# Latent layers with a couple's own projections between its rounds, and the first up-projections of three MLPs beside the last attention rounds

## The reference

```
attn = einsum(q, k) * scale, masked;  attn = softmax(attn)
out  = attn @ v @ out_w + out_b + residual
u    = rmsnorm(out, postnorm_w)              # layers 0 and 3
y    = gelu(u @ mlp_w1 + mlp_b1) @ mlp_w2 + mlp_b2 + residual
```

## Time and profile before

| | us |
|---|---|
| median of three runs | 2559.47 (2557.16 to 2562.12) |
| the profiled execution's own time | 2562.53 |
| its span | 2560.7 |
| PE busy in the span | 2452.8 |
| DVE, ACT, POOL busy | 1231.4, 1085.6, 1120.2 |

### The profile page before, as it was taken

The page is one execution under the profiler, slowest core; times in us unless marked ns, Lnnn a source line. Parts: engine busy times, 40 slices in busy tenths (PEclk is TensorE's granted clock), DMA queues, the critical chain, the costliest instruction groups (busy, mean ns, idle before and its releaser), DMA issues.

```text
span 2560.7 us, 48767 instructions
## 1 busy us (share of the span) xinstructions
PE 2452.8 (96%) x18464; PEld 2053.4 (80%) x18464; DVE 1231.4 (48%) x3296; ACT 1085.6 (42%) x3712; POOL 1120.2 (44%) x1972
## 2 busy tenths in 40 slices
PE   7999998999999999998888999999999999899999
PEld 6888886888888878886777788888888888788887
DVE  4555655332224667766666332243455556432332
ACT  4555554111114787777767111111455555311111
POOL 2453545600053787778876630033344443730000
PEclk9999999999999999998988999999999999999999
DMA  4111312211033233223443320122021111320100
GB/s 162 59 59 59 104 55 79 83 50 50 1 109 126 74 106 121 96 97 125 150 161 121 115 91 1 50 87 74 26 88 63 51 43 61 114 87 1 50 33 17
DMA packets 106774, 198.07 MB, mean 77 GB/s; under 512 B 8304, under 2 KB 35632, under 8 KB 103600
## 3 DMA queue, kind: packets, MB, share of 16 engines
q1 hardware_dynamic: 106544, 194.97, 23.1%
HBM read 136.22 MB, written 58.72 MB: 76 GB/s over the span
## 4 chain that ended last, share of the span: by engine, by line
PE 79%; ACT 11%; DVE 5%; POOL 3%; issue 1%; DMA 1%; SPq 0%; DVEq 0%; POOLq 0%
PE banks L326 70%; ACT plain_high L731 5%; PE banks L467 5%; PE banks L497 3%; ACT plain_low L731 2%; POOL plain_high L1342 2%; ACT plain_work L796 1%; DVE stats L1134 1%; PE banks L521 1%; ACT plain_work L715 1%; DVE plain_work L1149 0%; DMA plain_high<-attention_w 0%; DVE plain_high L1004 0%; ACT plain_low L715 0%; DVE rounded_low L1053 0%
## 5 line engine op out<-in xcount | busy, mean ns | idle before, releaser
L326 PE MATMUL banks<-rounded_work,rounded_low 128*128 128x512 f32 (+1 forms) x2688 | 534.3, 355 | 11.5 <-DVE rounded_low L1166 9.5
L326 PEld LDWEIGHTS banks<-rounded_work,rounded_low 128*128 128x128 f32 x2688 | 445.3, 198 | 76.8 <-issue 15.9
L982 ACT ACTIVATE plain_work<-banks,columns 128x512 f32<-128x512 f32 x192 | 132.4, 690 | 870.8 <-PE banks L326 870.8
L326 PE MATMUL banks<-rounded_work,rounded_high 128*128 128x512 f32 (+1 forms) x2400 | 483.4, 355 | 2.1 <-DMA rounded_work<-ctx_split 1.7
L326 PEld LDWEIGHTS banks<-rounded_work,rounded_high 128*128 128x128 f32 x2400 | 396.6, 191 | 68.2 <-issue 6.2
L1342 POOL TENSOR_SCALAR plain_high<-plain_high,inv_sum 128x128 f32<-128x128 f32 (+1 forms) x768 | 296.6, 409 | 317.5 <-DVE inv_sum L1026 317.2
L1318 DVE CAST rounded_work<-plain_work 128x512 fp32r<-128x512 f32 x192 | 105.3, 549 | 685.7 <-ACT plain_work L982 674.9
L326 PE MATMUL banks<-rounded_low,rounded_work 128*128 128x512 f32 x1728 | 414.9, 391 | 0.0
L326 PE MATMUL banks<-rounded_high,rounded_work 128*128 128x512 f32 (+1 forms) x1728 | 390.2, 377 | 0.0
L326 PEld LDWEIGHTS banks<-rounded_low,rounded_work 128*128 128x128 f32 x1728 | 321.6, 188 | 68.6 <-issue 2.8
L326 PEld LDWEIGHTS banks<-rounded_high,rounded_work 128*128 128x128 f32 x1728 | 309.1, 188 | 60.5 <-issue 1.4
(11 more groups left out here) (106 smaller groups left out, 3120.9 us busy)
## 6 DMA issues: line engine op xcount, KB each, us to landing
plain_work<-x SPq DMA_DIRECT2D x96, 256.0 KB, 3.2
plain_work<-mlp_w SPq DMA_DIRECT2D x96, 256.0 KB, 2.7
rounded_work<-ctx_split SPq DMA_DIRECT2D x16, 1024.0 KB, 6.0
u<-plain_work SPq DMA_DIRECT2D x48, 256.0 KB, 2.8
plain_work<-u SPq DMA_DIRECT2D x12, 1024.0 KB, 7.2
x<-plain_work SPq DMA_DIRECT2D x48, 256.0 KB, 2.3
plain_work<-attention_w SPq DMA_DIRECT2D x44, 256.0 KB, 2.6
ctx_split<-rounded_work SPq DMA_DIRECT2D x8, 1024.0 KB, 5.6
```

The costliest lines, as they stand in the source:

```text
L326: mm = pe.matmul(dst, lhs(i), rhs(j), start=first and n == 0, stop=last and n == 2, skip_group_check=True)
L982: act.activation(gelu[:, j % 2, :], bank(key), ACT.Gelu_apprx_tanh, bias=col(y, 28 + j)).then_inc(evac_of(key), 1)
```

## The change

- `Mlp` has a number `ahead`: 4 blocks in latent layers, 2 in layer 2. So many `up` blocks of the first group leave the MLP and are issued in the attention's last couple, with their GELU and their split. `up` becomes `pe_up`, the GELU `act_gelu`, the split `dve_split`; their waits are unchanged.
- In latent layers a couple's queries 1 and values 1 and 3 are made in its own time, between its rounds; only keys, queries 0 and values 0 and 2 are made in the couple before. The next couple's inputs and the output of sequence 2p-1 move from round 1 to round 2, on every engine. An attend waits only for the two values blocks that it reads.
- On POOL the last two norms and the root change places: norm of round 2 now stands ahead of the root of 2p-1 and, in the last couple, ahead of tiles 8 and 9. On SP the store of `u` for 2p-2 and the load of the next residual move to the head of a couple's list, ahead of the context and the stage.
- DVE's mask for the next couple moves ahead of round 3.
- `gelu` moves from 44 to 48 KB, where only `QT` lies.

```diff
-        gelu = work(plain, 44, 2, D)
+        gelu = work(plain, 48, 2, D)
...
-                for i in range(4 if y.kind == LATENT else 1):
+                for i in (b, 2 + b) if y.kind == LATENT else (0,):
                     wait_evac(pe, ("V", y.n, p, i))
...
                 pe_scores(pe, y, p, 1)
                 pe_turn_probs(pe, y, p, 0)
-                if more and y.n:
+                pe_queries(pe, y, p, 1)
+                pe_attend(pe, y, p, 0)
+                pe_values(pe, y, p, 1)
+                pe_values(pe, y, p, 3)
+                pe_scores(pe, y, p, 2)
+                pe_turn_probs(pe, y, p, 1)
+                if not more:
+                    pe_turn_u(pe, M[y.n], 0, 0)
+                    pe_turn_u(pe, M[y.n], 0, 1)
+                elif y.n:
                     pe_turn_x(pe, y, p + 1)
                 if p:
                     pe_out(pe, y, 2 * p - 1)
-                pe_attend(pe, y, p, 0)
+                pe_attend(pe, y, p, 1)
...
+                pe_scores(pe, y, p, 3)
+                pe_turn_probs(pe, y, p, 2)
+                if more:
+                    pe_queries(pe, y, p + 1, 0)
+                else:
+                    pe_up(pe, M[y.n], 0, 0)
                 pe_attend(pe, y, p, 2)
                 if more:
+                    pe_values(pe, y, p + 1, 0)
+                    pe_values(pe, y, p + 1, 2)
+                    pe_scores(pe, y, p + 1, 0)
+                else:
+                    pe_up(pe, M[y.n], 0, 1)
+                    pe_out(pe, y, 2 * p)
+                pe_turn_probs(pe, y, p, 3)
+                if more:
+                    pe_out(pe, y, 2 * p)
+                else:
+                    pe_up(pe, M[y.n], 0, 2)
+                pe_attend(pe, y, p, 3)
+                if more:
+                    pe_keys(pe, y, p + 1, 2)
                     pe_keys(pe, y, p + 1, 3)
...
+            pe_up(pe, M[y.n], 0, 3)
             pe_out(pe, y, B - 1)
...
                     pe_scores(pe, y, p + 1, 0)
+                else:
+                    pe_up(pe, M[y.n], 0, 0)
                 pe_turn_probs(pe, y, p, 1)
...
+            pe_up(pe, M[y.n], 0, 1)
             pe_out(pe, y, B - 1)
...
                     dve_keys(dve, y, p + 1, 1)
...
                     dve_mask(dve, y, p + 1)
-                    dve_values(dve, y, p + 1, 1)
-                dve_round(dve, y, p, 3, (p, 2), nothing)
...
+                    dve_split(dve, M[y.n], 0, 0)
+                    dve_out(dve, y, 2 * p)
+                dve_round(dve, y, p + 1, 0 if more else None, (p, 3), nothing)
...
+                pool_norm(pool, y, p, 2)
                 if p:
                     pool_root(pool, y, 2 * p - 1)
                 if not more:
                     pool_mlp_tiles(pool, y, 8, 10)
-                pool_norm(pool, y, p, 2)
                 pool_bias(pool, y, 2 * p)
...
+                if p:
+                    sp_store_u(sp, y, 2 * p - 2)
+                    sp_next_hidden(sp, y, 2 * p)
                 if not more:
                     sp_first_rows(sp, y)
```

More of the change, by code:

```diff
@@ L60, in __init__ @@
         self.m, self.y, self.g0, self.u0 = m, y, GROUPS * m, first_use
+        self.ahead = 2 if y.kind == CROSS else 4
 def build(nc, ins, out):
@@ L522, in pe_turn_u, with pe_up @@
             mm.then_inc(filled_by(key), 1)
+        def pe_up(pe, m, g, j):
+            y = m.y
+            if j == 0:
+                for f in range(FB):
+                    if y.kind == CROSS:
+                        pe.wait_ge(aff_split, 2 * PAIRS + FB * g + f + 1)
+                    else:
+                        wait_evac(pe, ("u", m.g0 + g, f))
+            if g == 0:
+                tiles_ready(pe, ("m", y.n), 2 * j)
+            key = ("h", m.g0 + g, j)
+            dst = begin(pe, key)
+            home = W[y.blocks[j]]
+            for f in range(FB):
+                mm = three_passes(pe, dst, lambda h: home[:, h * D + f * P:h * D + (f + 1) * P], lambda h: UT[:, h, f, :],
+                                  f == 0, f == FB - 1)
+            mm.then_inc(filled_by(key), 1)
         def pe_first_keys(pe, y):
@@ L543, in pe_latent @@
             pe_scores(pe, y, 0, 0)
-            pe_keys(pe, y, 0, 2)
-            pe_keys(pe, y, 0, 3)
-            pe_queries(pe, y, 0, 1)
-            for i in range(4):
+            for i in (2, 3):
+                pe_keys(pe, y, 0, i)
+            for i in (0, 2):
                 pe_values(pe, y, 0, i)
@@ L699, in pe_mlp @@
                 for j in range(NBLK):
-                    up(g, j)
+                    if g or j >= m.ahead:
+                        pe_up(pe, m, g, j)
                     if j >= 2:
@@ L818, in act_turn_u, with act_gelu @@
                 act.activation(UT[:, 0, f, :], bank(key), ACT.Copy, scale=col(y, 12 + f)).then_inc(hi_done, hi_count(key))
+        def act_gelu(act, m, g, j):
+            key = ("h", m.g0 + g, j)
+            wait_filled(act, key)
+            wait(act, g_ready, (m.g0 + g) * NBLK + j - 1)
+            act.activation(gelu[:, j % 2, :], bank(key), ACT.Gelu_apprx_tanh, bias=col(m.y, 28 + j)).then_inc(evac_of(key), 1)
         def act_round(act, y, p, k, turned, between, of=None):
@@ L868, in inputs @@
                 def inputs():
-                    if more and y.n:
+                    if not more:
+                        act_turn_u(act, M[y.n], 0, 0)
+                        act_turn_u(act, M[y.n], 0, 1)
+                    elif y.n:
                         act_x(act, y, p + 1, 0)
                         act_x(act, y, p + 1, 1)
-                    elif more:
+                    else:
                         act_stage(act, p + 1)
-                act_round(act, y, p, 1, (p, 0), inputs)
+                act_round(act, y, p, 1, (p, 0), nothing)
+                act_queries(act, y, p, 1)
                 act_heads(act, y, p, 0)
+                act_values(act, y, p, 1)
+                act_round(act, y, p, 2, (p, 1), inputs)
+                act_heads(act, y, p, 1)
                 if more:
@@ L973, in act_cross @@
                 act_heads(act, y, p, 1)
+            act_gelu(act, M[y.n], 0, 1)
         def act_mlp(act, m):
@@ L977, in act_mlp @@
             for g in range(GROUPS):
-                for j in range(NBLK):
-                    key = ("h", m.g0 + g, j)
-                    wait_filled(act, key)
-                    wait(act, g_ready, (m.g0 + g) * NBLK + j - 1)
-                    act.activation(gelu[:, j % 2, :], bank(key), ACT.Gelu_apprx_tanh, bias=col(y, 28 + j)).then_inc(evac_of(key), 1)
+                for j in range(0 if g else m.ahead, NBLK):
+                    act_gelu(act, m, g, j)
                 if g + 1 < GROUPS:
@@ L1306, in dve_mlp @@
                 gg = m.g0 + g
[L1307 to L1320 removed]
+                for j in range(0 if g else m.ahead, NBLK):
+                    dve_split(dve, m, g, j)
                 if g + 1 < GROUPS:
```

153 lines of the change are left out of this document (59 added, 94 removed).

## The result

The changed kernel takes 2546.4 us (median of six runs, 2542.7 to 2547.4) against 2558.9 of the kernel before on the same chip: a ratio of 0.9949, with a 95% interval of 0.9938 to 0.9959, so 10.5 to 15.9 us. The forecast of 2543.6 counted on 15.9 from 2559.5. The profiled execution of the changed kernel took 2544.39 us, with a span of 2542.4.

The account below looks back on a forecast made before the run. PE is busy 2452.8 of 2560.7 us, so only its idle or lower-clock time can be won. Gains of 7.4, 6.4 and 2.1 sum to 15.9 us: 2546.6 profiled, 2543.6 as median, range 2537 to 2553.

Parts of the forecast that it names:

- The bound: Ends of layers 0 and 3: after the change, POOL's list of tiles, splits and norms sets the end.
- The ends of layers 0 and 3, 13.7 us: Last rounds of both latent layers: up blocks and POOL's order shorten each to 38.3 us, gaining 7.4 and 6.4.
- charge of 1.7: Latent ends: one drop to half clock after the remaining idle time, 1.7 us in each; range allowed none or two.
- GELU and splits cost nothing there: Latent ends: ACT needs 0.7 us and DVE 1.1 per up block, under blocks of 2.7, so no cost.
- The steady couple, nothing: Middle couples of layers 0 and 3: no change in time; DVE's moved mask put at nothing, 0 to 0.5 us each.
- The end of layer 2, 2.1 us: Layer 2's last output: 3.7 us won ahead of it, 1.6 given back waiting before the fourth down block.
- The rival of the stretched norm: Latent ends: DVE's splits stretch POOL's last norm from 3.65 to 5.5 us, 1.8 per layer; 2547 us, chance 0.14.
- The other rivals: Steady clock, 2540 us, chance 0.14; bound not reached, about 2553, 0.09; late tile in steady couples, 2566, 0.06.
- PE's clock still drops: Judges the rival that PE's clock no longer drops: 1.7 us more won per latent end, 2540 us, chance 0.14.
- The bound was reached: Judges the rival that late POOL root or tile loads leave 2 us gain per latent end: about 2553, chance 0.09.
- No tile was late in steady couples: Judges the rival that POOL waits for a tile in layer 0's couples 1 to 4: 2566 us, slower, chance 0.06.
- the same instructions in another order: Steady latent couples: reordered projections leave about 12.2 us between a round's scores and its turning, so they cost nothing.

Follow-up runs that it names:

- e2: Changed kernel, with POOL's norm of round 3 ahead of tiles 8 to 11 in the last couple of layers 0 and 3: 2535.0 us.
- e5: Changed kernel, with POOL's norm of round 2 back behind the root and, in the last couple, tiles 8 and 9: 2565.8 us.
- e6: Kernel before, with only POOL's norms of rounds 2 and 3 moved ahead of tiles 8 to 11 in layers 0 and 3's last couple: 2546.8 us.
- e1: Changed kernel, with DVE's mask for the next latent couple moved behind round 3's probabilities: 2544.2 us, ratio 0.9950 to the kernel before.
- e9: Changed kernel, with POOL's norm of round 2 back behind the root and DVE's mask behind round 3's probabilities: 2558.5 us.
- e3: Changed kernel, with no up blocks issued ahead of any attention's end: 2565.8 us, ratio 1.0031 to the kernel before.
- e7: Changed kernel, with DVE's mask behind round 3's probabilities and POOL's last norm ahead of tiles 8 to 11: 2529.6 us.
- e10: Repeat of the changed kernel with mask behind round 3's probabilities and last norm ahead of tiles 8 to 11: 2533.7 us.
- e12: Changed kernel, with no up blocks ahead and POOL's last norm ahead of tiles 8 to 11: 2555.5 us, ratio 0.9991 to the kernel before.
- e8: Changed kernel, with mask moved back, last norm ahead of tiles, and layer 2's tiles 12 and 13 split behind the two last roots: 2532.0 us.
- e11: Repeat of the changed kernel with mask, last norm and layer 2's tiles 12 and 13 moved: 2530.8 us.

## Why the prediction was right, and where it wasn't

The median of 2546.4 us is 2.8 above the forecast and inside its range of 2537 to 2553. The mechanism of the two latent ends held; the term for the steady couple did not.

**The bound.** POOL's list at the two latent ends: shown, by e2, e5 and e6. Moving the last norm up removes the wait, moving the one of round 2 back makes one of 9.7 us.

**The ends of layers 0 and 3, 13.7 us.** The mechanism was right. In layer 0 the chain of times for POOL was right within 0.8 us, and the stretch within 0.1. In layer 3 the last norm came 1.7 us later than counted. The idle time was 3.8 and 4.7 us, where about 4 was predicted. Layer 3's stretch is 1.6 us longer, by 0.7 of wait and some 1.0 of half clock beyond the charge of 1.7, which the range had taken in. "GELU and splits cost nothing there" held for PE, but DVE's split 0 held up POOL's tiles by 0.6 and 0.7 us. The first and last stretches of the profile, with the MLPs, give 6.3 and 5.6 us, where 7.4 and 6.4 were predicted. In layer 0 the difference is the mask, 2.6 us, less 1.6 that the start of the layer won (granted clock 0.97 in the first 105 us, where it was 0.95 before); in layer 3 it is the 1.6 of its end, less 0.8 won ahead of it. For the 1.6 and the 0.8 that were won the change gives no reason: that is luck.

**The steady couple, nothing.** This is the step that failed, by a term that I had bounded with 0 to 0.5 us per couple and taken at 0: "the attend of round 2 behind it has some 0.5 us to spare by my reading". It had less, and the mask takes 0.79 us and not a few tenths beside POOL's addition. Six couples at 0.44 are 2.6 us; layer 3's were free, since its mask takes 0.28 to 0.37 us and no attend waits for it. With 1.6 us in layer 3's end and 1.0 in layer 2's, below, 5.2 us were missed, and 2.4 came back by luck, as told above. The medians show a miss of 3.4 (15.9 predicted, 12.5 measured, 10.5 to 15.9 by the interval).

**The end of layer 2, 2.1 us.** The mechanism was right in its waits. The size is 1.1 in most profiles: the new wait is 2.3 to 2.7 us where I had 1.6, and I had charged no half clock behind it, which costs 1.5 to 1.7 more. In e1, for one, 4.9 us are won ahead of that block, not 3.7, and 4.0 given back, not 1.6.

**The rival of the stretched norm.** It didn't come, 3.67 us in the changed kernel, for the reason given against it: split 0 was over at 425.17, before the norm began, and split 1 started at 433.72, behind it. How far splits would stretch it is open. In e5 and e9 layer 0's last norm met the start of a split and took 3.83 and 3.87 us, so 0.2 more and not 1.8. What did come is the opposite case, a DVE instruction that waits for POOL: the mask took 0.79 us beside an addition that had begun 0.63 us before it. In each of the cases above, and in layer 3 of the changed kernel, where it took 0.37 us, it ended 0.15 or 0.16 us after an instruction of POOL did. The Trainium skill (SBUF — State Buffer, Who interferes with whom) has both directions: of a VectorE instruction in a two-port mode and a GpSimd instruction, whichever comes first holds the shared port pair for its whole length, and the other waits. The trace agrees as to who waits; no run here shows in which mode the mask ran. I had looked only for POOL as the one that waits.

**The other rivals.** PE's clock still drops around the last wait, once in each layer, for 3.4 and 6.8 us. The bound was reached. No tile was late in steady couples: in layer 0 POOL waits 3.3 us for it and is still early, and no turning waits for POOL.

**What the count didn't hold.** I had put the whole gain on POOL's idle time and nothing on DVE's. e3 shows that the new order without the up blocks costs 8 us, some 2.6 for the mask and most of the rest at the ends, where DVE's copies then come late. In the changed kernel the up blocks cover that, down to 0.47 us, so the sum held; but "the same instructions in another order" cost nothing only with them.

## What to carry to other kernels

Before filling an engine's idle time with other work, look at what the engine that ends the wait does before it: here putting a norm ahead of four weight tiles was worth 9 us on either kernel. When steps move past each other, price the ones that seem too small to matter on the engine that every later step queues behind, and look at what POOL runs beside them if it is DVE. And read a small gain in the stretch where it arises: a change of 4 us in one place was plain in two profiles and invisible in the whole time.

## What the runs showed of the hardware that was not expected

- The same DVE instruction (a mask of 128x256, int32 to bf16, both in SBUF) took between 0.28 us and 1.86 us: 0.37, 0.79, 1.30 and 1.86 us in the places shown or told above, each time beside an instruction that POOL had begun before it. At 1.86 us it outlasted two POOL instructions in a row, though the second began only as the first ended; at 1.30 only one came.
- Layers 1 and 2 up to the last scores, the same code in all kernels, took 590.1 to 595.1 us in fourteen profiles, at a granted clock of 0.95 to 0.97. PE's busy time for the same instructions there went from 534.0 to 540.5 us: short waits are followed by half clock in some executions and not in others. Between e7 and e10, the same kernel, this stretch makes 4.3 of the 5.0 us between the two spans.
- A half-clock drop follows the waits: 5.46 us for an output block of 2.9 behind waits of 3.24 and 1.43 us (e12), 4.4 to 4.6 us for a down block of 2.9 behind single waits of 2.30 to 2.67 us in six profiles, no drop behind 1.66 us in a seventh, and none in the end of layer 0 once the longest wait is 0.6 us (e2).
- A wait can vanish because the engine got slower: in e8 and e11 half clock in the turning removed three waits and brought the attend behind them no earlier.
